# One-hot values on VectorE alone, another ScalarE order before the loop, and another spacing of the last expert tiles

## The chip, the cores and the metric

The kernel runs on one core of a Trainium2 chip. The metric is the device time of one execution in microseconds (us), as a median over runs. The engines are TensorE (PE in the profile, its weight loads PEld), VectorE (DVE), ScalarE (ACT), GpSimd (POOL) and SyncE (SP, which here only issues DMAs). An engine name with a q (ACTq, SPq) is that engine's sequencer as it issues DMAs.

## What is computed

A sequence of 4096 tokens with 256 channels is normalised, goes through a gated state-space layer (128 inner channels, 64 states each) and, beside it, through a mixture of 8 experts (two per token), and the two are multiplied onto a residual:

```python
xn = _layernorm(x, axis=-1)
s = _L0_attn_ref(xn, ...)      # up-projection, conv of 3 taps, silu, selective scan, gate, down-projection
g = _silu(_L0_ffn_ref(xn, gate, w1, w2, w3))  # top 2 of 8 experts, softmax weights
x = x + s * g
# the scan inside s, for each of 4096 steps:
h = dA * h + (d_t * u_t)[..., None] * b_t[:, None, :]
y = jnp.einsum('bdn,bn->bd', h, c_t)
```

## The kernel before

**Setup (0 to about 117 us).** The rows are normalised and stored (`xn_d`), transposed, and multiplied by the gate matrix. VectorE picks the two experts of each token and works out the slot of each (token, expert) pair in a list ordered by expert, with 128 slots to a tile: `slot_hi` names the tile, `slot_lo` the row in it. Tiles 0 to 63 always hold tokens; of tiles 64 to 70 only those that the routing fills do.

The list is inverted with one-hot matmuls in 16 batches of 4 blocks. For batch b, `one_hots(b)` (VectorE) makes two masks: `columns(b)`, the one-hot of `slot_lo` (L1014), and the one-hot of `slot_hi` (L1012). The second is needed twice, times the token number (`goal`) and times the routing weight (`prob`). For the batches 5, 7, 9, 11, 13 and 15 (`SHARED`) ScalarE makes these products, in `values_of_halves` (L725, L726, 8 instructions a batch); for the other ten VectorE does (L1018, L1019). `place_batch(b)` (TensorE, L1234) adds the products up in one bank. Masks live in two buffers, so that `one_hots(b)` waits for `place_batch(b - 2)`. When the 16th is in, `placed()` writes the index lists `dest` and `source`.

Between these, in an order written out by hand for each engine, runs the chain of the eight chunks of 512 tokens. For chunk c: ScalarE `scale_rows(c)` (L621), TensorE `transpose_y(c)` (L1147), ScalarE `evict_columns(c)` (L631), TensorE `left_right(c)` (L1201, in two halves, with `place_batch` calls between them), ScalarE `evict_halves(c)` (L639 to L642). On chunk 0 ScalarE also works out the first `delta` (`softplus`, L676 to L687), GpSimd sums it (L500 to L510), ScalarE rounds it (`high_part`, L692), GpSimd takes the rest (L515), SP stores the three (`store_parts`) and, once they have landed, loads `stack`. ScalarE's `load_delta(0)` waits for the same landing. TensorE's order is transpose 5, `left_right(4)`, batches 3 to 6, transpose 6, `left_right(5)`, batches 7 to 11, transpose 7, `left_right(6)`, batches 12 to 15, two `spread`s, `left_right(7)`.

**Loop (512 pairs of scans).** A pair is two inner channels by 64 states by 512 tokens. For each pair: TensorE spreads (`spread`, L1368), VectorE multiplies (L1064), ScalarE takes the exponential (L718), VectorE scans (L1073), GpSimd multiplies by C (L431), and TensorE reduces for every fourth pair (L1300). 64 pairs are a chunk, whose own work (`WORK_AFTER`) is spread over its first half and a little beyond.

The 71 expert tiles run in the same loop, placed by `turns_by_pair()`. A tile has one gather (POOL, L419), one transpose turn, four steps (TensorE L1352, ScalarE L740 and L742, VectorE L1085, GpSimd L446), four out turns (TensorE L1322), one `evict_out` (ScalarE L750) and one scatter-add (POOL, L455). A long tile takes LONG = 7 pairs, EXTRA of the 67 long ones take an eighth pair, and the last four take SHORT pairs each. For a tile that holds no token TensorE does a two-column matmul (L1287) in place of the turn's products (`if_live`); all the other engines do the same work as for a full tile. In this input tiles 67 to 70, the short ones, are the empty ones: with 18 and 4 they begin at pairs 488, 492, 496 and 500. GpSimd also adds a bias row to chunk 7 at pair 488 (`bias_rows`, L438).

**End.** When all scatter-adds have landed, SP loads six of the eight blocks of `results`. VectorE finishes the last gate and mixes and stores the rows.

Of the kernel before, what the change touches and what calls it, by code (L numbers as in the profile page):

```python
# [6 lines left out]
P = 128  # L7
# [16 lines left out]
BATCH = 4  # L24
# [12 lines left out]
SHARED = (5, 7, 9, 11, 13, 15)  # L37
LONG_TILES = 67
LONG, SHORT, EXTRA = 7, 4, 18
# [69 lines left out]
def mamba_and_experts(nc, x, gam, bet, w_up, b_up, conv_w, conv_b, w_dl, b_dl, w_b2, w_c2, a_log,  # L109
                      dvec, w_dn, b_dn, gate, w_all, c_ident, c_upper, c_pick, c_win, c_first,  # L110
                      c_start, c_token, out):
    with ExitStack() as ctx:
# [3 lines left out]
        def sem(name):  # L116
            return ctx.enter_context(nc.semaphore(name))
# [23 lines left out]
        iota = sb("iota", [P, P])  # L141
# [58 lines left out]
        def hots(b):  # L200

            home = ring[:, 8 + 2 * (b % 2):10 + 2 * (b % 2), :].rearrange("p a t -> p (a t)")
            return home[:, 0:BATCH * 2 * TILES].rearrange("p (n a h) -> p n a h", n=BATCH, a=2)
# [68 lines left out]
        s_equal, s_val, s_hot, s_perm, s_placed = (sem(k) for k in ("s_equal", "s_val", "s_hot", "s_perm", "s_placed"))  # L272
# [284 lines left out]
        def _(act):  # L557
# [163 lines left out]
            def values_of_halves(b):  # L721

                act.wait_ge(s_equal, b + 1)
                for n in range(BATCH):
                    act.activation(hots(b)[:, n, 0, :], hots(b)[:, n, 1, :], ACT.Identity, scale=blocks(goal, b)[:, n:n + 1])  # L725
                    ins = act.activation(hots(b)[:, n, 1, :], hots(b)[:, n, 1, :], ACT.Identity, scale=blocks(prob, b)[:, n:n + 1])  # L726
                ins.then_inc(s_val, 1)

# [15 lines left out]
            def evict_out(i):  # L744

                act.wait_ge(s_o, STEPS * (i + 1))
                if i == 0:
                    act.wait_ge(s_placed, 4)
                ge(act, s_res, 16 * i)
                act.activation(o_sb[:, i % 2, :], o_bank[:, 0:D], ACT.Identity, scale=weight[:, i:i + 1]).then_inc(s_oev, 1)  # L750
# [49 lines left out]
            evict_b(0)  # L800
            softplus(0, 2)
            softplus(0, 3)
            evict_columns(3)
            evict_halves(2)
            evict_c(0)
            scale_rows(4)
            high_part(0)
            evict_columns(4)
            scale_rows(5)
            evict_halves(3)  # L810
# [4 lines left out]
            values_of_halves(5)  # L815
            evict_halves(4)
            scale_rows(6)
            evict_columns(6)
            values_of_halves(7)
            scale_rows(7)  # L820
            values_of_halves(9)
            evict_halves(5)
            values_of_halves(11)
            evict_columns(7)
            values_of_halves(13)
# [4 lines left out]
            values_of_halves(15)  # L830
# [37 lines left out]
        def _(v):  # L868
# [137 lines left out]
            def one_hots(b):  # L1006

                v.wait_ge(s_slot, 1)
                ge(v, s_perm, b - 1)
                shape = [P, BATCH, TILES]  # L1010
                goals, weights = hots(b)[:, :, 0, :], hots(b)[:, :, 1, :]
                v.tensor_tensor(weights, blocks(slot_hi, b).unsqueeze(2).broadcast_to(shape),  # L1012
                                tiles[:, :].unsqueeze(1).broadcast_to(shape), ALU.is_equal).then_inc(s_equal, 1)
                ins = v.tensor_tensor(columns(b), blocks(slot_lo, b).unsqueeze(2).broadcast_to([P, BATCH, P]),  # L1014
                                      iota[:, :].unsqueeze(1).broadcast_to([P, BATCH, P]), ALU.is_equal)
                if b not in SHARED:
                    v.wait_ge(s_equal, b + 1)
                    v.tensor_tensor(goals, weights, blocks(goal, b).unsqueeze(2).broadcast_to(shape), ALU.mult)  # L1018
                    ins = v.tensor_tensor(weights, weights, blocks(prob, b).unsqueeze(2).broadcast_to(shape), ALU.mult)  # L1019
                ins.then_inc(s_hot, 1)  # L1020
# [120 lines left out]
        def _(pe):  # L1141
# [86 lines left out]
            def place_batch(b):  # L1228

                pe.wait_ge(s_hot, b + 1)  # L1230
                if b in SHARED:
                    pe.wait_ge(s_val, SHARED.index(b) + 1)
# [223 lines left out]
```

## Time and profile before

| | |
|---|---|
| median of three runs | 1339.98 us (1332.83 to 1341.99) |
| the profiled execution | 1335.25 us, its span 1333.4 us |
| busy in the span: PE, PEld | 1189.2, 912.7 us |
| busy: DVE, ACT, POOL | 1144.5, 774.7, 1102.1 us |
| first and last scan begin | 117.2 and 1303.3 us |
| mean granted TensorE clock | 0.952 |

A busy time is the union of an engine's instructions. A row of the timeline gives start, duration, engine, line, operation and tiles; consecutive like instructions are merged (x4), and in brackets stands how long the engine had been idle and what ended that. On DVE and ACT the next instruction can start some 0.1 us before the one before it is through, so costs are taken from start to start.

### The profile page before, as it was taken

How to read it: one execution, taken by the hardware profiler on the slowest of the kernel's cores; microseconds unless marked ns; L12 is line 12 of the kernel's file. 1: busy time of each engine (PE TensorE's matmuls, PEld its weight loads, DVE VectorE, ACT ScalarE, POOL GpSimd, SP SyncE). 2: the span in 40 equal slices, each digit the busy share in tenths (PEclk: the TensorE clock that was granted, in tenths of full speed). 3: DMA queues.
4: the chain of work that ended last, by engine and by line, in shares of the span. 5: the costliest groups of instructions: out<-in, count | busy, mean ns of one | idle time of the engine just before them, and what ended most of it. 6: DMA issues, size and time to landing. Idle time of an engine off the chain costs nothing. (4 is left out here: it accounts for less than half of the span.)

```text
span 1333.4 us, 26249 instructions
## 1 busy us (share of the span) xinstructions
PE 1189.2 (89%) x7740; PEld 912.7 (68%) x7740; DVE 1144.5 (86%) x1604; ACT 774.7 (58%) x1683; POOL 1102.1 (83%) x1029
## 2 busy tenths in 40 slices
PE   5878999998999999998999988998999989999781
PEld 4456777766777777776777766776677766777540
DVE  7756989988899979997899889897888978989887
ACT  6875665556554665566555755566544665545562
POOL 0022989889999988989998998799988987999997
PEclk8889999999999999999999999999999999999755
DMA  8433446554557446744574457444654457556647
GB/s 251 162 111 111 133 129 176 169 188 119 162 145 223 131 139 162 231 132 122 164 238 133 133 150 231 134 134 112 198 185 128 136 149 219 149 156 193 178 128 256
DMA packets 131214, 216.67 MB, mean 162 GB/s; under 512 B 14992, under 2 KB 49936, under 8 KB 131056
## 3 DMA queue, kind: packets, MB, share of 16 engines
q10 hardware_dynamic: 73728, 134.25, 33.3%
q1 hardware_dynamic: 43696, 61.96, 14.0%
q0 software_dynamic: 13632, 18.62, 8.1%
q8 instruction: 66, 1.08, 0.3%
q14 instruction: 92, 0.75, 0.2%
HBM read 186.47 MB, written 28.31 MB: 161 GB/s over the span
## 5 line engine op out<-in xcount | busy, mean ns | idle before, releaser
L431 POOL TENSOR_TENSOR arena<-arena,c_rep 128x512 f32<-128x512 f32 x512 | 689.8, 1393 | 74.9 <-DVE arena L1073 68.9
L1073 DVE TENSOR_TENSOR_SCAN arena<-bank,carry,arena 128x512 f32<-128x512 f32 x512 | 651.7, 1273 | 13.7 <-ACT bank L718 13.5
L1352 PEld LDWEIGHTS bank<-xgT,wring 128*128 128x128 f32 x4288 | 519.2, 194 | 118.9 <-issue 70.5
L1352 PE MATMUL bank<-xgT,wring 128*128 128x128 f32 x4288 | 538.8, 279 | 38.9 <-DMA wring<-in_w_all 17.2
L718 ACT ACTIVATE bank<-arena,a_neg 128x512 f32<-128x512 f32 x512 | 354.1, 692 | 99.9 <-DVE arena L1073 41.5
L1064 DVE TENSOR_TENSOR arena<-bank,b_rep 128x512 f32<-128x512 f32 x512 | 351.3, 686 | 30.5 <-PE bank L1368 7.6
L740 ACT ACTIVATE th<-bank 128x256 f32<-128x256 f32 x284 | 108.6, 382 | 348.0 <-PE bank L1352 323.7
L1322 PE MATMUL bank<-wring,hid 128*128 128x256 f32 x1072 | 274.0, 387 | 22.5 <-POOL hid L446 22.4
L1368 PE MATMUL bank<-stack,pick 128*128 128x512 f32 x512 | 272.9, 537 | 7.4 <-DVE arena L1064 7.4
L446 POOL TENSOR_TENSOR hid<-gt,ue 128x256 f32<-128x256 f32 x284 | 258.6, 911 | 16.7 <-DVE gt L1085 14.8
L1322 PEld LDWEIGHTS bank<-wring,hid 128*128 128x128 f32 x1072 | 193.4, 190 | 84.0 <-POOL hid L446 44.0
L1085 DVE SCALAR_TENSOR_TENSOR gt<-th,bank 128x256 f32<-128x256 f32 x284 | 114.7, 404 | 94.2 <-ACT th L740 72.5
L1300 PE MATMUL bank<-arena,win 128*32 128x512 f32 x1024 | 143.9, 635 | 7.4 <-POOL arena L431 7.4
L455 POOL DMA_INDIRECT results<-o_sb,dest x71 | 113.6, 1599 | 12.3 <-issue 10.4
L1368 PEld LDWEIGHTS bank<-stack,pick 128*128 128x128 f32 x512 | 100.2, 197 | 31.1 <-DVE arena L1064 17.8
L419 POOL DMA_INDIRECT xg<-xn_d,source x71 | 71.2, 1002 | 52.6 <-DVE source L1034 40.3
L742 ACT ACTIVATE ue<-bank 128x256 f32<-128x256 f32 x284 | 107.5, 378 | 0.8 <-POOL hid L446 0.7
L485 POOL TENSOR_TENSOR spare<-spare 128x512 f32<-128x512 f32 x8 | 12.9, 1607 | 55.6 <-ACT spare L670 55.6
L1300 PEld LDWEIGHTS bank<-arena,win 128*32 128x32 f32 x1024 | 20.6, 110 | 52.3 <-issue 34.6
L750 ACT ACTIVATE o_sb<-bank,weight 128x256 f32<-128x256 f32 x71 | 32.5, 458 | 9.2 <-PE bank L1322 6.8
L1335 PEld LDWEIGHTS bank<-ident,xg 128*128 128x128 f32 x134 | 16.7, 140 | 24.0 <-issue 11.6
L1287 PEld LDWEIGHTS bank<-ident 128*128 128x128 f32 x72 | 18.5, 311 | 21.1 <-issue 20.1
(183 smaller groups left out, 768.1 us busy)
## 6 DMA issues: line engine op xcount, KB each, us to landing
arena<-delta_d ACTq DMA_DIRECT2D x512, 256.0 KB, 3.8
wring<-in_w_all SPq DMA_DIRECT2D x64, 384.0 KB, 6.3
xn<-in_x SPq DMA_DIRECT2D x4, 1024.0 KB, 9.8
xn_d<-xn SPq DMA_DIRECT2D x4, 1024.0 KB, 5.4
results<-sr SPq DMA_DIRECT2D x4, 1024.0 KB, 11.1
parts_d<-spare SPq DMA_DIRECT2D x16, 256.0 KB
stack<-parts_d SPq DMA_DIRECT2D x16, 256.0 KB, 4.8
out<-arena SPq DMA_DIRECT2D x8, 512.0 KB, 3.0
```

The costliest lines, as they stand in the source:

```text
L431: pool.tensor_tensor(p_ring[:, s % P_RING, :], h_ring[:, s % H_RING, :], of_chunk(c_rep, c, 2), ALU.mult).then_inc(s_hc, 1)
L446: pool.tensor_tensor(hid[:, k % 4, :], gt[:, k % 2, :], ue[:, k % 2, :], ALU.mult).then_inc(s_hid, 1)
L455: pool.indirect_dma_start(results, bass.IndirectOffsetOnAxis(dest[:, i:i + 1], 0), o_sb[:, i % 2, :], None, compute_op=ALU.add).then_inc(s ...
L718: act.activation(a_bank[s % 2][:, :], dl_ring[:, s % D_RING, :], ACT.Exp, scale=a_neg[:, s % PAIRS:s % PAIRS + 1]).then_inc(s_exp, 1)
L740: act.activation(th[:, :], bank[:, 0:SW], ACT.Tanh, scale=0.5).then_inc(s_th, 1)
L1064: v.tensor_tensor(b_ring[:, s % B_RING, :], du_bank[s % 2][:, :], b_rep[:, cols(c)], ALU.mult).then_inc(s_bm, 1)
L1073: v.tensor_tensor_scan(out=h_ring[:, s % H_RING, :], data0=a_bank[s % 2][:, :], data1=b_ring[:, s % B_RING, :], initial=carry[:, q:q + 1], ...
L1085: v.scalar_tensor_tensor(out=gt[:, k % 2, :], in0=th[:, :], scalar=1.0, in1=bank_of((turn, i, j))[:, 0:SW], op0=ALU.add, op1=ALU.mult).the ...
L1300: ins = pe.matmul(y_bank[32 * g:32 * g + 32, :], win[:, 30 - 2 * i:62 - 2 * i], p_ring[:, (4 * q + g) % P_RING, :], start=False, stop=(i = ...
L1322: ins = pe.matmul(o_bank[:, 0:D], hid[:, k % 4, m * SLOT:(m + 1) * SLOT], wring[:, 2 * r + m, 4 * P:WROW], start=(r == 0 and m == 0), stop ...
L1352: ins = pe.matmul(bank[:, m * SW + r * SLOT:m * SW + (r + 1) * SLOT], wring[:, 2 * j + r, (2 * m + h) * P:(2 * m + h + 1) * P], xgT[:, i % ...
L1368: pe.matmul(du_bank[s % 2][:, :], pick[:, QUADS * (g % 2) + i16, :], stack[:, c % 2, g // 2, :], start=True, stop=True).then_inc(s_sel, 1)
```

## The change

1. `SHARED` and `values_of_halves` go. VectorE makes the products of all 16 batches, and TensorE no longer waits for `s_val`.
2. ScalarE's order before the loop is another one: `evict_columns(3)` and `scale_rows(4)` stand ahead of the last two parts of `softplus`, `high_part(0)` stands two calls later, and `scale_rows(6)` stands ahead of `evict_halves(4)`.
3. LONG, SHORT, EXTRA are 7, 5, 11 and were 7, 4, 18. The last four tiles begin at pairs 481, 486, 491 and 496, and the last out turn is at pair 502, where it was at 506.
4. `evict_out(i)` waits for the scatter-adds up to tile i - 2 and not up to i - 1; `o_sb` has two buffers.

```diff
-SHARED = (5, 7, 9, 11, 13, 15)
 LONG_TILES = 67
-LONG, SHORT, EXTRA = 7, 4, 18
+LONG, SHORT, EXTRA = 7, 5, 11
...
-            def values_of_halves(b):
-
-                act.wait_ge(s_equal, b + 1)
-                for n in range(BATCH):
-                    act.activation(hots(b)[:, n, 0, :], hots(b)[:, n, 1, :], ACT.Identity, scale=blocks(goal, b)[:, n:n + 1])
-                    ins = act.activation(hots(b)[:, n, 1, :], hots(b)[:, n, 1, :], ACT.Identity, scale=blocks(prob, b)[:, n:n + 1])
-                ins.then_inc(s_val, 1)
...
-                ge(act, s_res, 16 * i)
+                ge(act, s_res, 16 * (i - 1))
...
             softplus(0, 0)
             softplus(0, 1)
             evict_b(0)
+            evict_columns(3)
+            scale_rows(4)
             softplus(0, 2)
             softplus(0, 3)
-            evict_columns(3)
+            evict_c(0)
             evict_halves(2)
-            evict_c(0)
-            scale_rows(4)
-            high_part(0)
             evict_columns(4)
             scale_rows(5)
+            high_part(0)
             evict_halves(3)
             evict_columns(5)
             act.wait_ge(s_slot, 1)
             for s in range(D_RING - 1):
                 load_delta(s)
-            values_of_halves(5)
+            scale_rows(6)
             evict_halves(4)
-            scale_rows(6)
             evict_columns(6)
-            values_of_halves(7)
             scale_rows(7)
-            values_of_halves(9)
             evict_halves(5)
-            values_of_halves(11)
             evict_columns(7)
-            values_of_halves(13)
...
-            values_of_halves(15)
             evict_halves(6)
             evict_halves(7)
...
-                ins = v.tensor_tensor(columns(b), ...)
-                if b not in SHARED:
-                    v.wait_ge(s_equal, b + 1)
-                    v.tensor_tensor(goals, weights, ..., ALU.mult)
-                    ins = v.tensor_tensor(weights, weights, ..., ALU.mult)
-                ins.then_inc(s_hot, 1)
+                v.tensor_tensor(columns(b), ...)
+                v.wait_ge(s_equal, b + 1)
+                v.tensor_tensor(goals, weights, ..., ALU.mult)
+                v.tensor_tensor(weights, weights, ..., ALU.mult).then_inc(s_hot, 1)
...
                 pe.wait_ge(s_hot, b + 1)
-                if b in SHARED:
-                    pe.wait_ge(s_val, SHARED.index(b) + 1)
```

## Rows read from the trace of the kernel before

**Rows 1.** Windows: us, then busy time (instructions) by engine, PEclk, DMA share, GB/s.
```profile
117.00:1249.00 1132.00, 1057.42 (x7077) 827.85 (x7075) 1001.14 (x1267) 650.01 (x1408) 1017.90 (x960) 0.99 0.56 161
1249.00:1304.00 55.00, 39.09 (x135) 22.42 (x135) 47.40 (x63) 29.48 (x68) 52.74 (x49) 0.53 0.50 136
```

**Rows 2.** Timeline of TensorE in the setup.
```profile
65.83 1.04 PE L1147 MATMUL bank<-ident,wring 128*128 128x128 f32 x8
...
73.41 1.97 PE L1147 MATMUL bank<-ident,wring 128*128 128x128 f32 x8 [4.71 <-ACT wring L621]
...
90.79 1.09 PE L1147 MATMUL bank<-ident,wring 128*128 128x128 f32 x8 [0.79 <-ACT wring L621]
91.72 1.88 PE L1201 MATMUL bank<-arena,hid 128*128 128x512 f32 x4
...
113.76 1.21 PE L1234 MATMUL bank<-arena,o_sb 128*128 128x142 f32 x8 [0.71 <-ACT arena L726]
```

**Rows 3.** Timeline of ScalarE in the setup (ACTq: its DMA issues).
```profile
65.06 0.60 ACT L698 ACTIVATE b_rep<-bank 128x512 f32<-128x512 f32 x1 [1.40 <-PE bank L1226]
...
68.55 1.43 ACT L631 ACTIVATE arena<-bank,vec 128x512 f32<-128x512 f32 x2
...
71.63 1.72 ACT L621 ACTIVATE wring<-xn,rs 128x256 f32<-128x256 f32 x4
...
82.42 1.24 ACTq L711 DMA_DIRECT2D arena<-delta_d  x2
```

**Rows 4.** Timeline of VectorE in the setup, batches 1 and 3.
```profile
62.07 0.45 DVE L1012 TENSOR_TENSOR arena<-route,tiles 128x284 f32<-128x284 f32 x1
...
63.77 0.74 DVE L1043 TENSOR_TENSOR arena<-hid,arena 128x568 f32<-128x568 f32 x1
...
68.81 0.96 DVE L1012 TENSOR_TENSOR arena<-route,tiles 128x284 f32<-128x284 f32 x1 [0.52 <-PE bank L1234]
...
72.80 1.52 DVE L1019 TENSOR_TENSOR arena<-arena,route 128x284 f32<-128x284 f32 x1
```

**Rows 5.** Timeline of GpSimd and of SP's issues in the setup.
```profile
68.20 1.26 POOL L500 TENSOR_TENSOR spare<-spare 128x512 f32<-128x512 f32 x1 [8.63 <-ACT spare L684]
...
79.44 1.29 SPq L348 DMA_DIRECT2D stack<-parts_d  x2
```

**Rows 6.** The scans: count, ns min/median/max, first and last start.
```profile
L1073 DVE TENSOR_TENSOR_SCAN arena<-bank,carry,arena x512: 1259/1273/1283, 117.2 to 1303.3; 128x512 f32<-128x512 f32 x171
```

**Rows 7.** Timeline of VectorE at pairs 466, 473, 488, and among the last.
```profile
1203.30 1.27 DVE L1073 TENSOR_TENSOR_SCAN arena<-bank,carry,arena 128x512 f32<-128x512 f32 x1
...
1217.67 1.27 DVE L1073 TENSOR_TENSOR_SCAN arena<-bank,carry,arena 128x512 f32<-128x512 f32 x1
...
1248.94 1.27 DVE L1073 TENSOR_TENSOR_SCAN arena<-bank,carry,arena 128x512 f32<-128x512 f32 x1
...
1299.54 0.69 DVE L1064 TENSOR_TENSOR arena<-bank,b_rep 128x512 f32<-128x512 f32 x1
...
1301.53 0.69 DVE L1064 TENSOR_TENSOR arena<-bank,b_rep 128x512 f32<-128x512 f32 x1
```

**Rows 8.** Timeline of GpSimd in the stretch of the four empty tiles.
```profile
1250.50 2.35 POOL L438 TENSOR_TENSOR xn<-xn,bdn 128x1024 f32<-128x1024 f32 x1
...
1263.51 1.26 POOL L431 TENSOR_TENSOR arena<-arena,c_rep 128x512 f32<-128x512 f32 x1
1264.74 0.72 POOL L446 TENSOR_TENSOR hid<-gt,ue 128x256 f32<-128x256 f32 x1
...
1268.75 0.97 POOL L419 DMA_INDIRECT xg<-xn_d,source  x1 [0.16 <-issue]
...
1282.42 1.60 POOL L455 DMA_INDIRECT results<-o_sb,dest  x1 [0.17 <-issue]
1283.46 1.86 POOL L431 TENSOR_TENSOR arena<-arena,c_rep 128x512 f32<-128x512 f32 x1
```

**Rows 9.** The loads of delta (256 KB each), from issue to landing.
```profile
DMA to landing us min/median/max: 2.9/3.8/8.4
```

More of the change, by code:

```diff
@@ L271, in mamba_and_experts @@
         s_rt, s_rex, s_rex2, s_cnt, s_slot, s_table = (sem(k) for k in ("s_rt", "s_rex", "s_rex2", "s_cnt", "s_slot", "s_table"))
-        s_equal, s_val, s_hot, s_perm, s_placed = (sem(k) for k in ("s_equal", "s_val", "s_hot", "s_perm", "s_placed"))
+        s_equal, s_hot, s_perm, s_placed = (sem(k) for k in ("s_equal", "s_hot", "s_perm", "s_placed"))
         s_gatew, s_tapset = sem("s_gatew"), sem("s_tapset")
@@ L1013, in one_hots @@
                                 tiles[:, :].unsqueeze(1).broadcast_to(shape), ALU.is_equal).then_inc(s_equal, 1)
-                ins = v.tensor_tensor(columns(b), blocks(slot_lo, b).unsqueeze(2).broadcast_to([P, BATCH, P]),
-                                      iota[:, :].unsqueeze(1).broadcast_to([P, BATCH, P]), ALU.is_equal)
-                if b not in SHARED:
-                    v.wait_ge(s_equal, b + 1)
-                    v.tensor_tensor(goals, weights, blocks(goal, b).unsqueeze(2).broadcast_to(shape), ALU.mult)
-                    ins = v.tensor_tensor(weights, weights, blocks(prob, b).unsqueeze(2).broadcast_to(shape), ALU.mult)
-                ins.then_inc(s_hot, 1)
+                v.tensor_tensor(columns(b), blocks(slot_lo, b).unsqueeze(2).broadcast_to([P, BATCH, P]),
+                                iota[:, :].unsqueeze(1).broadcast_to([P, BATCH, P]), ALU.is_equal)
+                v.wait_ge(s_equal, b + 1)
+                v.tensor_tensor(goals, weights, blocks(goal, b).unsqueeze(2).broadcast_to(shape), ALU.mult)
+                v.tensor_tensor(weights, weights, blocks(prob, b).unsqueeze(2).broadcast_to(shape), ALU.mult).then_inc(s_hot, 1)
             def placed():
```

## Prediction

> **What bounds the kernel now.** I read the page first (busy times, then the costliest groups), then the windows, then engine by engine the timelines of the setup, of the empty tiles and of the end. The kernel has four stretches, each with a limit of its own.
>
> *The setup, to the first scan at 117.2 [rows 6].* The reader should look for what ends TensorE's idle time. It stands for 4.71 us until ScalarE has scaled the rows of chunk 4, again before transposes 6, and before the sixteenth batch it waits for ScalarE's products (L726) [rows 2]. So ScalarE's list sets the pace, though ScalarE has little to do that TensorE needs. From transposes 6 to the last batch TensorE takes 113.76 - 90.79 = 23.0 us.
>
> *The full tiles, pairs 1 to 487.* From 117.2 to 1248.94 [rows 6, 7] are 1131.7 us for 487 pairs, 2.32 us a pair. In the windows TensorE is busy for 93% of it, VectorE for 88%, GpSimd for 90% [rows 1]: three engines close to full, none all the time. What tells them apart is the length of a tile. The best seven-pair tile takes 1217.67 - 1203.30 = 14.37 us [rows 7]. A pair without a step takes VectorE 1301.53 - 1299.54 = 1.99 us [rows 7]; so one with a step takes (14.37 - 3 x 1.99) / 4 = 2.10. Dividing the 512 scan starts (first and last in [rows 6]) by tile gives a mean of 16.26 us for the 49 seven-pair tiles and 18.36 us for the 18 eight-pair ones: the eighth pair costs 2.10 us, with a standard error of 0.5, and the least lengths seen (14.37 and 16.35) give 1.98. The tile after an eight-pair one is no shorter than other seven-pair tiles (16.20 against 16.28), so the eighth pair doesn't serve others to catch up.
>
> *The empty tiles and the light pairs.* From 1248.94 to the last scan at 1303.3 [rows 6, 7] are 54.4 us for 23 pairs. GpSimd is busy for 52.7 of 55 us [rows 1], since an empty tile spares TensorE alone. TensorE's granted clock is 0.53 there, and near 1.0 in the full tiles [rows 1].
>
> *After the last scan* come some 30 us that follow from the last reduction; nothing of the change is in them.
>
> **The change, part by part.**
>
> *ScalarE's order and the values.* The six batches take 48 instructions off ScalarE. VectorE gets 12 more. One batch with its products costs VectorE 63.77 - 62.07 = 1.70 us [rows 4]; TensorE's matmuls of one take about 1.0 us (1.21 less the overlap) [rows 2], so with two buffers VectorE has each batch ready in time wherever TensorE has other work between.
>
> Step by step: `evict_columns(3)` can start when transposes 3 end, at 65.83 + 1.04 = 66.9 [rows 2]; it stood at 68.55 [rows 3]. It takes 1.34, `scale_rows(4)` 1.6 (both from [rows 3], less 0.1 of overlap), to 69.9. Transposes 4 start at 70.0 and not 73.41: 3.4 us early. What is put behind pays. The last parts of `softplus` began right behind `evict_b(0)` (65.06 [rows 3]), at 65.6, and now begin at 69.9, 4.3 us later. GpSimd's sums move from 68.20 to 72.5, and the landing of the three stores, seen where SP goes on to the stack, from 79.44 to 83.8 [rows 5]. Behind this stands ScalarE itself: it gets to `load_delta(0)`, by 3.0 for softplus, 0.5, 1.3, 1.34, 1.6, 1.3 and 1.34 (softplus and `evict_c` as the gaps between its rows, `evict_halves` 1.3), at 81.5 and waits to 83.8, where it issued at 82.42 without a wait [rows 3]. Three issues cost 1.9, then `scale_rows(6)` 1.7: transposes 6 at 87.5, not 90.79, 3.3 us early. From there TensorE has its own list: two transposes at 0.93, four half products at 1.75, eight batches at 1.0, together 16.9, and 0.9 us of waiting before batch 11, where three batches follow each other and VectorE's 1.70 shows: 17.8 us where it took 23.0. Batch 15 starts at 105.3, not 113.76: **8.5 us early**. The list indices, the first gather, `left_right(7)` and the loop hang on it with fixed distances. Weights and stack, 4.4 us later on SP, are wanted only after 105. Bounds: without the wait in `load_delta` the gain is 8.5 + 2.3 = 10.8. If a batch of VectorE's runs against GpSimd as batch 3 did, it takes 72.80 + 1.52 - 68.81 = 5.5 us [rows 4], 3.8 more than 1.70, and the gain is 4.7. I take 8.5, as the sums on GpSimd (72.5 to 78.4) meet batch 4 alone and TensorE wants that at 81.
>
> A rule of the Trainium skill speaks against the new products. Batch 3 took 5.5 us and not 1.7 just while GpSimd's sums ran from 68.20 on [rows 4, 5]. The page "SBUF — State Buffer", section "SBUF: two separate sides", has a VectorE instruction with two SBUF inputs and a GpSimd instruction that reads SBUF exclude each other for the whole instruction. The trace agrees with it in the batch of 5.5 us. By that rule batch 4 would hold GpSimd's sums up as well, which is the second rival below.
>
> *Seven pairs out of the full tiles.* 7 x 1.98 = 13.9 to 7 x 2.10 = 14.7; I take **14.3 us** less.
>
> *Empty tiles of five pairs, and three more light pairs.* GpSimd's sum over the four tiles from [rows 8]: 20 pairs at 1.23 (1264.74 - 1263.51) = 24.6; 16 step products at 0.70 = 11.2; two gathers at 0.97 + 0.16 = 2.3; four scatter-adds at 1.04 + 0.17 = 4.8; the bias row 2.3; 45.2 us. The same sum for 16 pairs is 40.3. Then came six light pairs at 1.99 and the last scan 1.2 behind its forerunner, 13.1, together 53.4 where 54.4 were measured: 1.0 us goes to waits. New: 45.2 + 1.0, and from pair 501 nine times 1.99 and 1.2, 19.1: 65.3 us, **10.9 us more**. Bounds: below, VectorE's own pace, 16 x 2.10 + 4 x 1.99 = 41.6 in place of 46.2, so 6.3 more; above, GpSimd adds the waits in proportion, 1.3 more, and 12.2.
>
> *The wait of `evict_out`.* At full tiles the scatter-add has landed a tile's length before; nothing is gained, and VectorE, two exponentials ahead, covers the one wait in the light pairs. 0. *Results loaded earlier:* the last out turn is at pair 502, so 3 MB are loaded while the last deltas come in. A delta has three pairs, 6.0 us, and took 3.8 in the middle and 8.4 at most [rows 9]: between 0 and 2.4 us; I take 0.5.
>
> Sum: -8.5 - 14.3 + 10.9 + 0.5 = **-11.4 us**. The profiled execution took 1335.25 us, 4.7 below the median 1339.98 of the three runs; I put the difference on both. Span 1333.4 - 11.4 = 1322.0; time 1339.98 - 11.4 = **1328.6 us**. About 1% (13.4 us, to 1326.6 and 1353.4) is what a measurement of this kernel can tell from no change.
>
> **The rivals.**
>
> *VectorE sets the pace of the empty tiles.* With five pairs to a tile GpSimd's hold loosens, and the four take 41.6: -8.5 - 14.3 + 6.3 + 0.5 = -16.0, 1324.0. For it: GpSimd's backlog can ride in the eight buffers of the scans. Against it: the step products are in order behind the bias row and TensorE waits for them.
>
> *GpSimd and VectorE block each other in the setup.* Gain 4.7 there: -7.6, 1332.4. For it: the 5.5 us of batch 3 [rows 4]. Against: only batch 4 meets the sums.
>
> *The loop's start doesn't move,* because something I hold for covered (weights, stack, the first gather) ends last: -2.9, 1337.1. Against: weights and stack are there some 10 us before they are wanted, and the gather moves with the lists.
>
> *The removed pairs come back as waits (slower).* TensorE is busy for 93% of the full tiles [rows 1] and does the same turns in seven pairs less. If it is what holds them, a tile takes as long with seven pairs as with eight, the 14.3 us aren't gained and the 10.9 are still paid: -8.5 + 10.9 + 0.5 = +2.9, 1342.9. It decides from where a removed pair saves less than 0.41 us. Against it: 2.10 and 16.20 above.
>
> **How the numbers follow.** Forecast 0.45 (its own spread 1325 to 1332, a quarter of it below 1326.6), VectorE's pace 0.20, blocking 0.15, no earlier start 0.12, waits come back 0.08. The range from 1320 to 1338 takes in the first four with their bounds and leaves out the last and the ends, under 2 in 10. Faster by over 1%: 0.20 + 0.11 = 0.31. Slower by over 1% needs the last rival and a late start together: 0.03. Within 1%: 0.66.
>
> **What the new profile would show.** Transposes 4 at 70 and transposes 6 at 87.5; a gap on ScalarE up to 83.8; the first scan at 108.6; no idle time of TensorE on L726. Pair 481 (the first empty tile) some 1117 us behind the first scan; from there 65 us to the last scan, with GpSimd the fuller engine; 30 us after it. The prediction is wrong if the first scan comes after 113, if the 67 full tiles take 16.9 us each as now (I expect 1117 / 67 = 16.7), or if the empty tiles take over 50.

## The result

| | before | changed |
|---|---|---|
| median of 6 runs each, side by side | 1337.61 us | 1326.95 us |
| ratio, 95% interval | | 0.9927 (0.9907 to 0.9948) |
| ratio in a second comparison, same kernel | | 0.9944 (0.9925 to 0.9963) |
| profiled execution, its span | 1335.25, 1333.4 us | 1330.77, 1329.0 us |
| first and last scan | 117.2, 1303.3 us | 109.4, 1299.2 us |

The change saves 0.6 to 0.7% of the time, some 9 us (9.8 and 7.5 us by the two ratios). The forecast was 11.4 us, under 1%. As a time it was 1328.6 us and the measured median is 1326.95 us; part of that closeness is luck, since the median of the kernel before was 1337.61 us here and 1339.98 us in the runs that the forecast started from. The profiled execution of the changed kernel was the slowest of its six, so its span understates the gain; below I use several profiles.

The scans of the changed kernel (line L1056, as the lines have moved), then its windows, in the columns of [rows 1]; they answer to [rows 6] and [rows 1]:

```profile
L1056 DVE TENSOR_TENSOR_SCAN arena<-bank,carry,arena x512: 1259/1273/1284, 109.4 to 1299.2; 128x512 f32<-128x512 f32 x171
```
```profile
109.40:1233.40 1124.00, 1049.64 (x7054) 827.25 (x7052) 989.75 (x1253) 646.77 (x1402) 1010.02 (x954) 0.99 0.57 160
...
1232.80:1299.20 66.40, 46.02 (x158) 24.27 (x158) 60.31 (x76) 34.20 (x75) 61.27 (x55) 0.52 0.63 177
```

The first scan is 7.7 us earlier. Beside that, the reader sees a stretch of full tiles that is as mixed as before (TensorE busy for 93%, GpSimd for 90%, VectorE for 88%), and an end in which GpSimd is no longer busy all the time.

**The setup.** Timeline of TensorE in the changed kernel; it answers to [rows 2]. The lines are transposes 4, transposes 5, the first half of `left_right(4)`, transposes 6, batches 11 and 15:

```profile
70.36 1.09 PE L1130 MATMUL bank<-ident,wring 128*128 128x128 f32 x8 [1.30 <-ACT wring L620]
...
78.05 1.31 PE L1130 MATMUL bank<-ident,wring 128*128 128x128 f32 x8 [2.19 <-ACT wring L620]
79.16 3.39 PE L1184 MATMUL bank<-xgT,hid 128*128 128x512 f32 x4
...
88.24 1.03 PE L1130 MATMUL bank<-ident,wring 128*128 128x128 f32 x8
...
97.57 1.24 PE L1215 MATMUL bank<-arena,o_sb 128*128 128x142 f32 x8 [0.72 <-DVE arena L1003]
...
106.01 1.24 PE L1215 MATMUL bank<-arena,o_sb 128*128 128x142 f32 x8
```

Transposes 4 wait 1.30 us and not 4.71 for ScalarE; transposes 6 wait for nobody; batch 11 shows the one short wait for VectorE; batch 15 starts 7.75 us before its place in [rows 2]. Timeline of ScalarE at `load_delta` (L710) and `scale_rows(6)` (L620), which answers to the last of [rows 3]:

```profile
83.67 2.17 ACTq L710 DMA_DIRECT2D arena<-delta_d  x3
85.89 1.71 ACT L620 ACTIVATE wring<-xn,rs 128x256 f32<-128x256 f32 x4 [4.46 <-issue]
```

ScalarE stood still for 4.46 us, about half of it for the stored deltas and half to issue the three loads. Batch 4 on VectorE against the sums on GpSimd, which answers to [rows 4, 5]:

```profile
75.96 1.03 DVE L997 TENSOR_TENSOR arena<-route,tiles 128x284 f32<-128x284 f32 x1 [5.01 <-PE bank L1215]
76.91 1.75 DVE L999 TENSOR_TENSOR xg<-route,iota 128x512 f32<-128x512 f32 x1
78.59 0.44 DVE L1002 TENSOR_TENSOR arena<-arena,route 128x284 f32<-128x284 f32 x1
78.95 1.52 DVE L1003 TENSOR_TENSOR arena<-arena,route 128x284 f32<-128x284 f32 x1
```
```profile
72.84 1.27 POOL L499 TENSOR_TENSOR spare<-spare 128x512 f32<-128x512 f32 x1 [12.97 <-ACT spare L683]
...
75.42 1.26 POOL L505 TENSOR_TENSOR spare<-spare 128x512 f32<-128x512 f32 x1
76.76 1.35 POOL L509 TENSOR_TENSOR spare<-spare 128x512 f32<-128x512 f32 x1
...
78.86 1.30 POOL L514 TENSOR_TENSOR spare<-spare 128x512 fp32r<-128x512 f32 x1 [0.74 <-ACT spare L691]
```

The batch takes 80.47 - 75.96 = 4.5 us where it takes 1.7 alone. GpSimd's instructions take 1.26 to 1.35 us all the same: here VectorE pays for the meeting, GpSimd hardly.

**The end.** VectorE at pair 481, the first empty tile, and at two light pairs; then SP's loads of the results, in the changed kernel. They answer to [rows 7]:

```profile
1233.38 1.27 DVE L1056 TENSOR_TENSOR_SCAN arena<-bank,carry,arena 128x512 f32<-128x512 f32 x1
...
1293.44 0.69 DVE L1047 TENSOR_TENSOR arena<-bank,b_rep 128x512 f32<-128x512 f32 x1
...
1295.42 0.69 DVE L1047 TENSOR_TENSOR arena<-bank,b_rep 128x512 f32<-128x512 f32 x1
```
```profile
1290.35 6.30 SPq L370 DMA_DIRECT2D wring<-results  x6
```

From 1233.38 to the last scan at 1299.2 are 65.8 us. The loads of 3 MB begin at 1290.35, nine microseconds before the last scan, and the light pairs keep their pace beside them: 1295.42 - 1293.44 = 1.98 us. The last load of delta was issued at 1290.18, just before them.

### The profile page after: what moved, and what is told of

Its sections match the earlier page's. It is cut to its first block, busy times and chain, and to the rows that moved or that the text cites. A ratio compares the mean times of both kernels' runs of the same rounds, so it can differ in the third digit from the quotient of the medians.

```text
span 1329.0 us, 26206 instructions
## 1 busy us (share of the span) xinstructions
PE 1188.8 (89%) x7740; PEld 915.1 (69%) x7740; DVE 1149.4 (86%) x1616; ACT 763.1 (57%) x1635; POOL 1102.2 (83%) x1029
## 4 chain that ended last, share of the span: by engine, by line
PE 57%; POOL 18%; issue 10%; DVE 6%; DMA 5%; ACT 3%; SPq 1%; ACTq 1%; POOLq 0%; DVEq 0%
PE bank L1333 25%; PE bank L1303 12%; POOL arena L430 8%; PE bank L1281 6%; PE bank L1349 5%; POOL hid L445 5%; DMA wring<-in_w_all 5%; PE bank L1184 2%; POOL results L454 2%; DVE arena L1056 2%; POOL xg L418 1%; PE bank L1215 1%; PE bank L1209 1%; PE bank L1290 1%; ACT th L731 1%
## 5 line engine op out<-in xcount | busy, mean ns | idle before, releaser
L1056 DVE TENSOR_TENSOR_SCAN arena<-bank,carry,arena 128x512 f32<-128x512 f32 x512 | 651.9, 1273 | 21.1 <-ACT bank L717 21.0
L731 ACT ACTIVATE th<-bank 128x256 f32<-128x256 f32 x284 | 108.8, 383 | 347.9 <-PE bank L1333 322.7
L1349 PE MATMUL bank<-stack,pick 128*128 128x512 f32 x512 | 276.9, 544 | 10.0 <-DVE arena L1047 10.0
L1268 PEld LDWEIGHTS bank<-ident 128*128 128x128 f32 x72 | 17.8, 309 | 24.3 <-issue 23.6
## 6 DMA issues: line engine op xcount, KB each, us to landing
results<-sr SPq DMA_DIRECT2D x4, 1024.0 KB, 11.4
```

Source lines behind the costliest of these rows:

```text
L731: act.activation(th[:, :], bank[:, 0:SW], ACT.Tanh, scale=0.5).then_inc(s_th, 1)
L1056: v.tensor_tensor_scan(out=h_ring[:, s % H_RING, :], data0=a_bank[s % 2][:, :], data1=b_ring[:, s % B_RING, :], initial=carry[:, q:q + 1], ...
L1349: pe.matmul(du_bank[s % 2][:, :], pick[:, QUADS * (g % 2) + i16, :], stack[:, c % 2, g // 2, :], start=True, stop=True).then_inc(s_sel, 1)
```

## The experiments

This table has the stretches of all profiles with the kernel's full work, one profile each, from the starts of the scans. "Full" is from the first scan to that of the first empty tile, "end" from there to the last scan. Times are in us; the ratio is to the kernel before on the same chip.

| kernel | spacing | first scan | full (pairs) | end | ratio (95%) |
|---|---|---|---|---|---|
| before | 7, 4, 18 | 117.2 | 1131.8 (488) | 54.4 | |
| before_again | 7, 4, 18 | 118.0 | 1135.1 (488) | 54.7 | 0.9986 (0.9967 to 1.0005) |
| setup_only | 7, 4, 18 | 109.7 | 1132.6 (488) | 54.6 | 0.9940 (0.9923 to 0.9957) |
| values_only | 7, 4, 18 | 112.4 | 1133.7 (488) | 54.0 | 0.9967 (0.9946 to 0.9987) |
| order_only | 7, 4, 18 | 119.6 | 1138.7 (488) | 54.0 | 1.0026 (1.0000 to 1.0052) |
| changed | 7, 5, 11 | 109.4 | 1124.0 (481) | 65.8 | 0.9927 (0.9907 to 0.9948) |
| after_again | 7, 5, 11 | 108.8 | 1122.3 (481) | 65.8 | 0.9944 (0.9925 to 0.9963) |
| tiles_only | 7, 5, 11 | 117.2 | 1126.2 (481) | 65.8 | 0.9997 (0.9979 to 1.0015) |
| short4_extra11 | 7, 4, 11 | 110.0 | 1118.1 (481) | 67.2 | 0.9957 (0.9938 to 0.9976) |
| short6_extra4 | 7, 6, 4 | 110.1 | 1106.5 (474) | 80.8 | 0.9930 (0.9904 to 0.9956) |
| better | 7, 5, 14 | 111.6 | 1118.1 (484) | 59.6 | 0.9875 (0.9854 to 0.9897) |

### The halves of the change: setup_only, tiles_only, and both kernels again

```diff
 # setup_only: the changed kernel, but
-LONG, SHORT, EXTRA = 7, 5, 11
+LONG, SHORT, EXTRA = 7, 4, 18
-                ge(act, s_res, 16 * (i - 1))
+                ge(act, s_res, 16 * i)
```

> The values on VectorE and ScalarE's new order, with the old tile spacing and the old wait of evict_out. My theory (the setup hangs on ScalarE's list, and nothing later takes the lead back): the first scan comes at 109.4 us as in the changed kernel, and the time is 7.7 us below before, ratio 0.994. Rival (the loop gives part of it back, because weights and deltas now land while the loop already runs): first scan at 109.4, but the stretch from the first to the last scan longer than 1186 us by some microseconds, ratio 0.996 to 1.000.

Measured: first scan at 109.7, first to last scan 1187.2 us (1186.2 and 1189.8 in the two profiles of before), ratio 0.9940. The theory holds: the whole lead of the setup, 8.0 us by the ratio, is there at the end, and the loop gives nothing back.

```diff
 # tiles_only: the kernel before, but
-LONG, SHORT, EXTRA = 7, 4, 18
+LONG, SHORT, EXTRA = 7, 5, 11
```

> Only the spacing of the tiles (7, 5, 11 for 7, 4, 18); setup and waits as before. My theory (a pair taken out of the full tiles saves 1.98 to 2.10 us, the end grows by 10.9): the time is 2.9 us below before, ratio 0.998; from the pair of the first empty tile to the last scan 65.3 us. Rival (the removed pairs come back as waits on TensorE): that stretch is 65 us too, but pairs 0 to 481 take over 1122 us, and the time is 0 to 8 us above before.

Measured: ratio 0.9997 (0.9979 to 1.0015), so between 2.8 us less and 2.0 us more; my 2.9 us less lie just outside. The end took 65.8 us, as both said. The full tiles took 1126.2 us, more than the 1122 from which I had given the rival right. Yet that is 5.6 us less for 481 pairs than the first profile of before had for 488: part of what the removed pairs should have given is missing, not all. (This profiled execution, 1341.08 us, was 3.8 us slower than the median of its kernel's runs.)

> The kernel before, unchanged, for a second profile and as the zero of this comparison. Both theories: ratio 1.000, the interval shows what a comparison can tell. If the profiles of one kernel differ by several microseconds in the full tiles alone (pairs 0 to 487 took 1131.8 us in the first profile), then the 7.8 us that the two profiles show there, in place of 14.3, is the spread of single executions; if they agree within 1 us, the removed pairs were worth less than I took them for.

> The changed kernel, unchanged, for a second profile. My theory: pairs 0 to 481 take some 1117 to 1120 us (1124.0 in the first profile, whose execution was the slowest of six), the end from pair 481 65.8 us again, first scan at 109.4, ratio to before 0.992. Rival (the removed pairs are worth 1.1 us each): 1124 us again in pairs 0 to 481.

Measured: two profiles of before differ by 3.3 us in the full tiles, two of the changed kernel by 1.7 us. So the 1124.0 us of the first profile weren't an accident of that execution, and the 1117 to 1120 us that I expected of the second did not come (1122.3). Four profiles with 481 pairs give 1122.7 us on average, five with 488 pairs 1134.4: seven pairs are worth 11.7 us, with a standard error of 2.1 (by the spread within each group), 1.7 us a pair. The end grew by 65.8 - 54.3 = 11.5 us. What is gained in the full tiles is given back at the end. The timed runs of tiles_only say the same without any profile of the full tiles: the time changed by -0.4 us and the end by +11.5, so the full tiles gave 11.9 us (between 9.5 and 14.3, by the interval of the ratio).

### The halves of the setup: values_only and order_only

```diff
 # values_only: setup_only, with ScalarE's old order (values_of_halves left out)
+            softplus(0, 2)
+            softplus(0, 3)
             evict_columns(3)
-            scale_rows(4)
-            softplus(0, 2)
-            softplus(0, 3)
...
-            scale_rows(6)
             evict_halves(4)
+            scale_rows(6)
```

> All products on VectorE, but ScalarE's old order (the calls of values_of_halves simply left out), old tile spacing and wait. My theory (two delays in series: scale_rows(4) and scale_rows(6) hold TensorE up to its transposes 6 at 90.8, the values after it): transposes 6 stay at 90.7 to 91, the 23.0 us from there to the last batch become 17.8, so the first scan comes at 112.0, 5.2 us early, ratio 0.996. Rival (the products were the only brake): first scan at 109.5, ratio 0.994.

```profile
73.85 1.97 PE L1130 MATMUL bank<-ident,wring 128*128 128x128 f32 x8 [4.71 <-ACT wring L620]
...
91.16 1.09 PE L1130 MATMUL bank<-ident,wring 128*128 128x128 f32 x8 [0.90 <-ACT wring L620]
...
108.99 1.24 PE L1215 MATMUL bank<-arena,o_sb 128*128 128x142 f32 x8
```

This is TensorE of values_only, transposes 4, transposes 6 and batch 15. The wait of 4.71 us at transposes 4 is back to the hundredth, transposes 6 stand at 91.16, and from there to batch 15 are 17.8 us and no longer 23.0. First scan at 112.4 (112.0 expected), ratio 0.9967 (0.996 expected): two delays in series, and the rival's 109.5 is out.

```diff
 # order_only: the kernel before with the new order; its values stay where they were
+            evict_columns(3)
+            scale_rows(4)
             softplus(0, 2)
...
                 load_delta(s)
+            scale_rows(6)
             values_of_halves(5)
             evict_halves(4)
-            scale_rows(6)
             evict_columns(6)
             values_of_halves(7)
```

> ScalarE's new order, but with the products of six batches still on ScalarE in their old places between the calls; old tile spacing and wait. My theory: transposes 6 at 87.5 to 88.2 as in the changed kernel, 23 us from there to the last batch as before, first scan 2.6 to 3.3 us early at 114, ratio 0.998. Rival (ScalarE's wait for the stored deltas, 2 to 4 us, falls in front of the first products and takes the gain back): first scan at 116 to 117, ratio 1.000.

Both expectations missed. The first scan came at 119.6, 2 us after that of before. Timeline of TensorE in order_only at batches 5 and 6 and transposes 6, then of ScalarE at the three loads of delta and `scale_rows(6)`:

```profile
88.48 2.23 PE L1234 MATMUL bank<-arena,o_sb 128*128 128x142 f32 x8 [3.49 <-ACT arena L726]
90.50 2.10 PE L1234 MATMUL bank<-arena,xg 128*128 128x142 f32 x8
92.39 1.91 PE L1147 MATMUL bank<-ident,wring 128*128 128x128 f32 x8
```
```profile
82.46 2.17 ACTq L711 DMA_DIRECT2D arena<-delta_d  x3
84.67 1.70 ACT L621 ACTIVATE wring<-xn,rs 128x256 f32<-128x256 f32 x4 [4.45 <-issue]
```

ScalarE stands for 4.45 us in `load_delta`, does `scale_rows(6)`, and only then the products of batch 5. Batch 5 comes before transposes 6 in TensorE's list, so TensorE waits 3.49 us, and its next matmuls take twice their time (2.23 against 1.24 us). So the new order pays only where no product hangs behind the loads of delta: alone it costs 2.2 us (119.6 against 117.4, the mean of three profiles with the old setup), on top of the other half it brings 112.4 - 109.3 = 3.1 us (109.3 is the mean of the first three profiles with both halves; with the later ones they lie between 108.8 and 110.1).

Other profiles show what holds transposes 6 in the changed kernel, and it isn't what I had forecast. `scale_rows(6)` ends at 85.89 + 1.71 = 87.60, as forecast (87.5), but TensorE only gets to transposes 6 at 88.24, since it had stood for 2.19 us before transposes 5 and was slow behind that pause. In short6_extra4, which has the same setup, the pause is as long but the matmuls behind it take 1.88 us and not 3.39, and there transposes 6 do wait for ScalarE, 0.95 us. Timeline of TensorE in short6_extra4, transposes 5, the first half of `left_right(4)` and transposes 6:

```profile
79.21 1.09 PE L1130 MATMUL bank<-ident,wring 128*128 128x128 f32 x8 [2.20 <-ACT wring L620]
80.14 1.88 PE L1184 MATMUL bank<-xgT,hid 128*128 128x512 f32 x4
...
88.83 1.09 PE L1130 MATMUL bank<-ident,wring 128*128 128x128 f32 x8 [0.95 <-ACT wring L620]
```

From transposes 5 to transposes 6 are 9.6 us there and 10.2 in the changed kernel: the slow stretch cost 0.6 us in the end, and the rest of it fell into time in which TensorE would have waited.

### The price of a pair at the end: short4_extra11 and short6_extra4

```diff
 # both: the changed kernel, but
-LONG, SHORT, EXTRA = 7, 5, 11
+LONG, SHORT, EXTRA = 7, 4, 11
 # and the other
+LONG, SHORT, EXTRA = 7, 6, 4
```

> The changed kernel with four pairs for each of the last four tiles and 11 tiles with an eighth: the empty tiles at pairs 481 to 497, then 15 light pairs. Theory (in the empty tiles GpSimd is the bound, a pair there costs its 1.23 us, a light pair costs VectorE's 1.99): the end from pair 481 takes 41.3 + 13 x 1.99 + 1.2 = 68.4 us, 2.6 more than with five pairs each (65.8), and the full tiles 1124 as with five; ratio 0.995 to 0.996. Rival (VectorE is the bound in the empty tiles too): the end takes 65.8 us as with five pairs.

> The changed kernel with six pairs for each of the last four tiles and 4 tiles with an eighth (first empty tile at pair 474, last out turn at 498). After the runs with the spacing alone I hold two prices against each other. Price of the prediction, 2.04 us a removed pair: pairs 0 to 474 take 1133 - 28.6 = 1105 us, the end from pair 474 76 us, 6 to 7 us less than with the old spacing: ratio 0.989. Price from the profiles so far, 1.29 us a pair (1133.2 us for 488 pairs against 1124.2 for 481, means of three profiles each): 1115 us for pairs 0 to 474, end 76 us, 3.6 us more than the old spacing: ratio 0.997.

With four pairs the end took 67.2 us, 40.2 in the empty tiles and 27.0 in the light pairs; with five pairs 65.8, 46.5 and 19.3. Four pairs more in the empty tiles cost 6.3 us, 1.6 a pair, between GpSimd's 1.23 and VectorE's 1.99. So five pairs beat four, by 1.4 us at this place (2.6 expected). With six pairs the end took 80.8 us where I had 76. The 24 pairs of the empty tiles took 55.8 us of it. By the prices of the prediction VectorE needs 49.5 us for them and GpSimd 50.1, and in that stretch they were busy for 49.4 and 51.9 us: neither alone is the bound. On top come waits of VectorE at one step in each of the four tiles, 5.4 us in all; this is the longest, at the third step of tile 67:

```profile
1224.91 0.42 DVE L1068 SCALAR_TENSOR_TENSOR gt<-th,bank 128x256 f32<-128x256 f32 x1 [2.84 <-ACT th L731]
```

Against 1134.4 us for 488 pairs the 14 pairs of short6_extra4 saved 27.9 us, 2.0 each, and at the end they cost 26.5. So pairs 0 to 474 came as the prediction's price had them (1106.5 us, 1105 expected, where the lower price had 1115), and the end was what I had too short. Its ratio of 0.9930 is that of the change.

### Which engine holds the full tiles: pe_less, pool_less, dve_less

```diff
 # pe_less: one of the two products of each out turn
-                    for m in range(2):
+                    for m in range(1):
...
-                                        ..., stop=(r == STEPS - 1 and m == 1), ...)
+                                        ..., stop=(r == STEPS - 1), ...)
 # pool_less: GpSimd's product of a step on half the width from the third tile on
+                w = SW if k < 8 else SLOT
-                pool.tensor_tensor(hid[:, k % 4, :], gt[:, k % 2, :], ue[:, k % 2, :], ALU.mult)
+                pool.tensor_tensor(hid[:, k % 4, 0:w], gt[:, k % 2, 0:w], ue[:, k % 2, 0:w], ALU.mult)
 # dve_less: VectorE's product of a pair on 320 of 512 columns from the ninth pair on
-                v.tensor_tensor(b_ring[:, s % B_RING, :], du_bank[s % 2][:, :], b_rep[:, cols(c)], ALU.mult).then_inc(s_bm, 1)
+                w = CH if s < 8 else 320
+                v.tensor_tensor(b_ring[:, s % B_RING, 0:w], du_bank[s % 2][:, 0:w], b_rep[:, c * CH:c * CH + w], ALU.mult).then_inc(s_bm, 1)
```

> The changed kernel with half of the products of each out turn left out (one of two slices of the hidden values; the result lacks the other): in the full tiles 67 x 4 x 2 passes of 0.21 us, 114 us, less work for TensorE, all turns and waits kept. It asks which engine holds the full tiles (pairs 0 to 481, 1122 to 1126 us in three profiles, where VectorE's least is 2.05 us a pair, 986 us). Theory VectorE: the stretch shortens by under 30 us. Rival TensorE (the removed pairs were worth less than 2.04 us because TensorE has the same turns in less time): by 60 us and more.

> The changed kernel with GpSimd's product of each step on half the width from the third tile on (the other half keeps old values): 0.35 us less for each of 268, 94 us less work for GpSimd. If GpSimd holds the full tiles, pairs 0 to 481 shorten by 50 us and more, and the end from pair 481 by 16 x 0.35 = 5.6 us; if it is VectorE or TensorE, the full tiles shorten by under 25 us and the end by little.

> The changed kernel with VectorE's product of each pair on 320 of 512 columns from the ninth pair on (the others keep old values): 0.23 us less for each, 108 us less in pairs 8 to 481. If VectorE holds the full tiles they shorten by 80 to 108 us and a light pair goes from 1.99 to 1.76; if TensorE and GpSimd hold them too, by 60 us or less in the full tiles, and still 0.2 us a light pair.

| less work for | by about | full tiles, pairs 0 to 481 | shorter than 1122.7 by |
|---|---|---|---|
| TensorE | 114 us | 1099.0 us | 24 us |
| GpSimd | 94 us | 1106.7 us | 16 us |
| VectorE | 108 us | 1111.4 us | 11 us |

There is one profile of each. Two profiles of one kernel differ by 2 to 3 us, and three with the setup and the first 481 pairs of the changed kernel by 5.9 (1118.1 to 1124.0), so the order of GpSimd and VectorE in this table isn't shown. These are the windows of pe_less, pool_less and dve_less (each from near its first scan to about pair 483, 480 and 479), in the columns of [rows 1]:

```profile
109.00:1214.00 1105.00, 962.51 (x6531) 730.86 (x6529) 991.55 (x1259) 645.64 (x1406) 1011.65 (x959) 0.98 0.57 163
```
```profile
109.00:1214.00 1105.00, 1044.71 (x7049) 827.90 (x7048) 987.00 (x1251) 644.64 (x1398) 938.89 (x952) 0.99 0.56 162
```
```profile
109.00:1218.00 1109.00, 1046.48 (x7041) 827.56 (x7040) 902.71 (x1250) 643.97 (x1396) 1005.36 (x950) 0.99 0.56 161
```

The work did go: the engine's busy time falls by some 70 to 90 us in each. The stretch falls by an eighth to a little over a quarter of that. No single engine holds the full tiles, and so not VectorE either, on whose pace the prediction had built its price of a pair. The end, from pair 481, fell from 65.8 to 63.7 us in pool_less, where GpSimd as the only bound would have given 5.6 us: it isn't the only bound there. Where VectorE alone is the bound, in the light pairs, its shorter product shows in full, as here in dve_less, 1278.91 - 1277.13 = 1.78 us a pair and no longer 1.99:

```profile
1277.13 0.49 DVE L1048 TENSOR_TENSOR arena<-bank,b_rep 128x320 f32<-128x320 f32 x1
...
1278.91 0.49 DVE L1048 TENSOR_TENSOR arena<-bank,b_rep 128x320 f32<-128x320 f32 x1
```

### A version that beats both: better

```diff
 # the changed kernel, but
-LONG, SHORT, EXTRA = 7, 5, 11
+LONG, SHORT, EXTRA = 7, 5, 14
             scale_rows(4)
+            scale_rows(5)
+            evict_columns(4)
+            evict_halves(2)
             softplus(0, 2)
             softplus(0, 3)
             evict_c(0)
-            evict_halves(2)
-            evict_columns(4)
-            scale_rows(5)
-            high_part(0)
             evict_halves(3)
             evict_columns(5)
+            scale_rows(6)
+            high_part(0)
+            evict_halves(4)
+            evict_columns(6)
+            scale_rows(7)
             act.wait_ge(s_slot, 1)
             for s in range(D_RING - 1):
                 load_delta(s)
-            scale_rows(6)
-            evict_halves(4)
-            evict_columns(6)
-            scale_rows(7)
             evict_halves(5)
```

> The changed kernel with a further step in the same directions: on ScalarE scale_rows(5) directly behind scale_rows(4), evict_columns(4) and evict_halves(2) ahead of the last parts of softplus, scale_rows(6), evict_columns(6) and scale_rows(7) ahead of the three loads of delta; tiles 7, 5, 14 (first empty tile at pair 484, last out turn at 505). Theory (TensorE's remaining wait of 2.2 us at transposes 5 and its half clock behind it go; VectorE then has to make two batches against GpSimd's sums): first scan at 107 us, 2.4 us earlier than in the changed kernel, and the end no later; loop as before it; ratio 0.991 to 0.992 against 0.9935 for the change. Rival (the stored deltas, now 4 us later, hold the stack or the loads up): first scan at 110 or later, ratio 0.995.

Measured: 1320.86 against 1335.54 us, ratio 0.9875 (0.9854 to 0.9897), so faster than the change as well, whose two ratios are 0.9927 and 0.9944. But not for the reason I gave. The setup is worse, first scan at 111.6. TensorE of this kernel, transposes 5 and batches 5 and 6; then VectorE in batch 5, and the last of GpSimd's sums:

```profile
75.63 1.03 PE L1130 MATMUL bank<-ident,wring 128*128 128x128 f32 x8
...
83.73 1.24 PE L1215 MATMUL bank<-arena,o_sb 128*128 128x142 f32 x8 [1.68 <-DVE arena L1003]
86.49 2.26 PE L1215 MATMUL bank<-arena,xg 128*128 128x142 f32 x8 [1.53 <-DVE arena L1003]
```
```profile
80.12 1.75 DVE L999 TENSOR_TENSOR o_sb<-route,iota 128x512 f32<-128x512 f32 x1
81.80 1.51 DVE L1002 TENSOR_TENSOR arena<-arena,route 128x284 f32<-128x284 f32 x1
```
```profile
81.40 1.59 POOL L509 TENSOR_TENSOR spare<-spare 128x512 f32<-128x512 f32 x1
```

Transposes 5 lost their wait and came 2.4 us earlier, as meant. But GpSimd's sums slid to 77.0 to 83, with the rest behind them to 85.2, and now meet three batches of VectorE's. TensorE waits for two of them and runs batch 6 and what follows at up to half speed (batch 6 takes 2.26 us against 1.24, transposes 6 take 1.92 against 1.03, the four matmuls behind them 2.93 against 1.88). So transposes 6 start at 88.55, where the changed kernel has them at 88.24, and batch 7 at 93.0 where it has it at 90.8: these 2.2 us are the whole delay of the first scan (111.6 against 109.4). The rival had the first scan as late, but through another mechanism, loads that hold the setup up, which these rows don't show. The gain is in the loop: the full tiles took 1118.1 us for 484 pairs, where the line between 1122.7 at 481 and 1134.4 at 488 has 1127.7; the end took 59.6 us, where the prices of the prediction give 59.3. Those 10 us in the full tiles I did not expect. Nor are they the scatter of one profile, since the five timed runs put this kernel 7 to 9 us ahead of the change. Setup and spacing were changed together, so their cause isn't shown. That it is the spacing is likely: setup_only and before, with different setups and one spacing, differ by 1 us from the first to the last scan, and the first 64 pairs take 145.0 us in all five profiles with 18 eight-pair tiles, whatever the setup, 147.4 to 147.9 in the four with 11, and 145.6 here. The 1118.1 us of short4_extra11 don't support it: its first 481 pairs are those of the changed kernel, and its profiled execution (1327.21 us) was the fastest of its ten, 4.2 us below their median. One thing more goes along with the gain: in the full tiles the granted clock was 1.00 in this profile and 0.98 to 0.99 in the others, and in the 33 timed runs of before beside short4_extra11 those with a higher mean clock were mostly the faster ones (as 1333.4 us at 0.955 and 1345.8 us at 0.944). Whether the clock is cause or effect, no run shows.

## Why the prediction was right, and where it was off

The time moved the way that was forecast, by two thirds to seven eighths of the amount (7.5 and 9.8 us of 11.4). By parts, each from the mean of its profiles:

| part | forecast | measured |
|---|---|---|
| first scan | -8.5 | 117.4 to 109.3: -8.1 |
| full tiles, seven pairs fewer | -14.3 | 1134.4 to 1122.7: -11.7 (standard error 2.1) |
| end, from the first empty tile | +10.9 | 54.3 to 65.8: +11.5 |
| results loaded while deltas come in | +0.5 | not apart from the end |
| sum | -11.4 | -8.3; by the two ratios -9.8 and -7.5 |

- *ScalarE's list sets the pace of the setup.* Right, and shown from two sides: without the new order the wait of 4.71 us is back, without the moved products (order_only) TensorE waits again for ScalarE's products (L726) before five batches, 8.7 us in all, and with them moved alone (values_only) the 23.0 us from transposes 6 to batch 15 are 17.8. Step by step: transposes 4 at 70.4 (70.0 forecast), load of delta from 83.7 (83.8), transposes 6 at 88.2 (87.5), 17.8 us from there to batch 15 (17.8), first scan 109.4 (108.6). Two steps were not as forecast. The wait of 2.19 us before transposes 5 and the slow matmuls behind it were not in the sum, and it is they, not `load_delta`, that place transposes 6; that both come out within 0.7 us of each other is luck. And ScalarE's list up to `load_delta(0)` adds up, by the terms that the prediction gives, to 80.3 and not 81.5 (`high_part`, 0.6 us, has no term); it measured 81.4, and nothing hung on it, as the landing came at 83.7.
- *Weights, stack and gather covered.* Right: TensorE began the first step of the first tile 4.5 us behind the first scan before and after.
- *Blocking in the setup.* The meeting of batch 4 and the sums came as forecast and cost VectorE 2.8 us. That rival's outcome, a later chain on GpSimd, did not come: the sums took 5.3 us against 5.8 before. The Trainium skill ("SBUF — State Buffer", section "SBUF: two separate sides") has whichever of the two starts first hold the other off for its whole instruction. The trace agrees for VectorE: its slowed instructions end at 76.99, 78.66 and 80.47, each 0.3 to 0.6 us behind the end of a GpSimd instruction (76.68, 78.11, 80.16). GpSimd lost less, 0.1 us here and 0.3 us at most in the kernel before and in better (1.59 against 1.26 us). That doesn't speak against the rule, since VectorE's own instructions are the shorter ones (0.45 to 0.68 us alone), but it makes the price one-sided.
- *The price of a removed pair, 2.04 us.* This is the term that was off. The mean lengths of seven- and eight-pair tiles in one profile (2.10 apart) looked like its measurement. In the two profiles of the changed kernel the same means are 3.1 apart. This is not the scatter of executions: all four profiles with 11 eight-pair tiles have 3.0 to 3.2, all five with 18 have 2.0 to 2.2. So the comparison depends on which tiles have the eighth pair; that their place in a chunk does it is likely and not shown. With seven pairs really taken out it is 1.7 us, with fourteen 2.0, and the run `better` shows some 10 us that hang on the spacing or on the setup and not on the number of pairs. The standard error of 0.5 us a pair that stood beside the 2.10, 3.5 us for seven, covers the miss of 2.6 us; so the size is off by no more than the prediction allowed, but its ground, that a pair costs VectorE's 1.98 to 2.10 us, is refuted by dve_less (11 us for 108 us less work).
- *The empty tiles.* Right: 46.5 us to pair 501 where 46.2 were forecast, 19.3 behind it where 19.1 were. That GpSimd alone is the bound there was too strong: a pair more cost 1.6 us and not 1.23, and pool_less took off 2.1 us and not 5.6.
- *VectorE's pace in the empty tiles* (the rival with 41.6 us) and *removed pairs come back as waits* are refuted, the first by 46.5 us, the second by the 1.7 us: it needed under 0.41. Part of it came true all the same, the 2.6 us that are missing from the full tiles.
- *Results loaded earlier.* The overlap that I gave 0.5 us hardly exists. The last delta was issued at 1290.18, before the first load of results at 1290.35, and of the earlier ones only the one before it, issued at 1288.19, was still on its way; it landed after 3.9 us, where the median of the whole run is 3.7.
- *The wait of `evict_out`.* In the changed kernel `evict_out` no longer waits for a scatter-add at all, and the light pairs run at the same 1.98 us. No run changed it alone, but tiles_only keeps the old wait with the new spacing, and its end is the same 65.8 us: it is worth nothing, as forecast.

## What to carry to other kernels

In a hand-ordered setup, write down for each engine what the critical engine waits for, and move what nobody waits for (here ScalarE's products and the softplus) behind it or off that engine; check what a moved piece drags with it, here a chain over two engines and a DMA back to a blocking wait on the first. Where three engines are each nine tenths busy, don't price work at one engine's rate: about a hundred microseconds less for any one of them gave 11 to 24. A mean over groups within one profile is no price either, if the groups lie at different places; change the number and profile that. And before a profile is used, see where its execution lies among the timed runs: here the profiled ones were up to 4 us off their medians, as much as what was to be explained.

## What the runs showed of the hardware

- A VectorE product that ran beside GpSimd's took three times as long (1.52 against 0.45 us at 128x284), while GpSimd's grew by 6% here (1.35 against 1.27 us at 128x512) and by up to 25% in the kernel before and in better (1.59 us). I had left it open which of the two pays.
- TensorE often ran the matmuls behind a pause at about half speed: 3.39 us for four where four others took 1.88 (2.19 us of pause), 2.23 us for a batch that takes 1.24 (3.49 us of pause), 2.26 us for such a batch in better (1.53 us of pause, with another of 1.68 shortly before). A pause so can cost more than its length. In the changed kernel the granted clock was 1.00 from 68.7 to 75 us and 0.81 on average from 75 to 81, so for part of that time at 1.2 and not 2.4 GHz; TensorE had stood still for 2.19 us just before 78.05. But the length of the pause alone doesn't decide: behind the pause of 2.20 us in short6_extra4 the same four took 1.88 us at a granted clock of 1.00, and behind the 1.30 us before 70.36 there is no loss either.
- Six loads of results, 3 MB, issued from 1290.35 on, left VectorE's light pairs at 1.98 us. What they do to a load of delta isn't shown: one alone, issued at 1288.19, has a recorded landing beside them (3.9 us; 3.7 in the median of the run).
